# Output projections of two attention loops in three passes of high and low parts, next to the value projection

## The reference, cut to what matters

```python
x = x + tanh(g_xattn[0]) * L0_xattn(layernorm(x), ctx)      # q from x, k and v from ctx; W_proj, b_proj
x = x + tanh(g_ffn[0])   * L0_ffn(layernorm(x))             # top-1 of 8 experts, capacity, gelu
x = x + tanh(g_xattn[1]) * L1_xattn(layernorm(x), ctx, ctx) # wq, wk, wv, wo
x = x + tanh(g_ffn[1])   * L1_ffn(layernorm(x))             # top-2 of 4 experts
```

## Time and profile before

| | us |
|---|---|
| median of 3 runs | 2356.29 (2355.44 to 2358.41) |
| profiled execution | 2359.46 |
| its span | 2357.7 |
| PE busy | 2199.6 (93%) |
| DVE busy | 1744.6 (74%) |
| POOL busy | 1228.8 (52%) |
| ACT busy | 1193.6 (51%) |

### The profile page before, as it was taken

One profiled execution on the slowest core, in us unless ns is written; L12 is line 12 of the kernel. 1 busy time (PEld: TensorE's weight loads), 2 busy tenths in 40 slices (PEclk: granted clock), 3 DMA queues, 4 the chain that ended last, 5 costly groups with the idle time before them and its releaser, 6 DMA issues.

```text
span 2357.7 us, 55177 instructions
## 1 busy us (share of the span) xinstructions
PE 2199.6 (93%) x18512; PEld 1816.8 (77%) x18512; DVE 1744.6 (74%) x4727; ACT 1193.6 (51%) x2389; POOL 1228.8 (52%) x2200
## 2 busy tenths in 40 slices
PE   4999999999599999999969999999789999999997
PEld 3887787787488888888858888888667777777775
DVE  2788888888456666575558877878668888888885
ACT  2655555555333332333336666666556656666663
POOL 2666776776300000000056666666258888888886
PEclk9999999999799999999979999999989999999998
DMA  8112122112212222221122222222200000000000
GB/s 265 44 60 64 57 62 64 57 62 89 110 36 92 87 80 92 74 91 38 45 70 68 69 72 71 67 67 91 93 12 28 28 28 27 27 28 31 27 23 17
DMA packets 125388, 148.06 MB, mean 63 GB/s; under 512 B 13834, under 2 KB 117522, under 8 KB 122772
## 3 DMA queue, kind: packets, MB, share of 16 engines
q1 hardware_dynamic: 119060, 128.84, 17.0%
q0 software_dynamic: 6144, 16.79, 2.2%
HBM read 86.86 MB, written 58.72 MB: 62 GB/s over the span
## 4 chain that ended last, share of the span: by engine, by line
PE 73%; DVE 9%; POOL 8%; issue 4%; ACT 2%; SPq 2%; DMA 1%; POOLq 0%; ACTq 0%; DVEq 0%
PE ps L1095 11%; PE ps L974 10%; PE ps L1109 8%; PE ps L959 5%; PE ps L1039 5%; PE ps L913 4%; PE ps L1111 4%; PE ps L1058 4%; PE ps L1177 4%; DVE u2g L1481 3%; PE ps L1006 3%; PE ps L930 2%; PE ps L1132 2%; PE ps L907 2%; DVE h_st L1450 2%
## 5 line engine op out<-in xcount | busy, mean ns | idle before, releaser
L1229 DVE TENSOR_REDUCE nmax<-ps 128x16 f32<-128x2048 f32 x128 | 293.3, 2291 | 62.0 <-PE ps L930 61.9
L826 ACT ACTIVATE hid<-ps,b_in 128x512 f32<-128x512 f32 x192 | 132.5, 690 | 361.6 <-PE ps L1095 338.7
L592 POOL COPY slot_in<-slot_all 128x1 int32 (+1 forms) x64 | 11.4, 178 | 567.6 <-DMA eo_d<-eo 567.6
L784 ACT ACTIVATE prob_t<-ps 128x2048 f32<-128x2048 f32 x128 | 240.5, 1879 | 76.9 <-PE ps L913 76.9
L1109 PE MATMUL ps<-w_hl,hid_hi 128*128 128x512 f32 x768 | 269.5, 396 | 0.0
L1095 PE MATMUL ps<-xgt_hi,w_hl 128*128 128x512 f32 x768 | 243.8, 394 | 1.5 <-DVE xgt_lo L1382 1.5
L1177 PE MATMUL ps<-w2f,a_t 128*128 128x256 f32 x1024 | 244.2, 382 | 0.0
L1177 PEld LDWEIGHTS ps<-w2f,a_t 128*128 128x128 f32 x1024 | 196.3, 192 | 27.7
L1111 PE MATMUL ps<-w_hl,hid_lo 128*128 128x256 f32 x768 | 212.9, 277 | 0.0
L863 ACT ACTIVATE z<-ps,h_rs 128x256 f32<-128x256 f32 x256 | 123.7, 563 | 165.4 <-POOL h_rs L696 165.4
L566 POOL TENSOR_TENSOR km_r<-qk,cst 128x512 fp32r<-128x512 f32 x128 | 133.4, 1042 | 130.1 <-ACT qk L774 130.0
(11 more groups left out here) (196 smaller groups left out, 6038.5 us busy)
## 6 DMA issues: line engine op xcount, KB each, us to landing
c_t<-in_ctx_in_dram SPq DMA_DIRECT2D x128, 128.0 KB, 2.1
x_d<-x SPq DMA_DIRECT2D x128, 128.0 KB, 2.1
w_raw<-in_w_dram SPq DMA_DIRECT2D x16, 1024.0 KB, 7.9
slots_d<-zeros SPq DMA_DIRECT2D x12, 1024.0 KB, 9.3
xg<-slots_d SPq DMA_DIRECT2D x24, 512.0 KB, 4.7
eo_d<-eo SPq DMA_DIRECT2D x24, 512.0 KB, 3.2
x_in<-in_x_dram SPq DMA_DIRECT2D x64, 128.0 KB, 2.1
x_in<-x_d SPq DMA_DIRECT2D x64, 128.0 KB, 2.3
```

The costliest lines, as they stand in the source:

```text
L784: nc.scalar.activation(prob_t[:].rearrange("p a k -> p (a k)"), scores.rearrange("p a k -> p (a k)"), ACT.Exp, scale=SOFT).then_inc(y["exp ...
L826: nc.scalar.activation(hid[:, fc % 2, :], ps[:, 4 + fc % 2, 0:G], ACT.Gelu, bias=b1_in[:, e.parity, fc:fc + 1]).then_inc(z["hid_done"].sem, 1)
L1229: nc.vector.tensor_reduce(nmax[:, b.parity, :, 0:4], scores.rearrange("p a (r k) -> p a r k", k=P), AX_X, ALU.max, negate=True).then_inc(y ...
```

## The change

The output projection takes high and low parts in float32r, in three passes, as the value projection does. In both loops:

- ACT makes `o_hi` behind `o_t`, from the same PSUM bank; POOL makes `o_lo = o_t - o_hi` behind the bias (loop 0) or the gather (loop 1), ahead of `km_r`. PE waits for `o_lo` in place of `o_t`.
- PE's output projection stands behind the turning of `xh`, directly ahead of the value projection, and has six matmuls.
- POOL's `c_lo` moves from ahead of `km_r` and `qm` to behind them, ahead of the scatter.
- `w_v` and `w_p` share one buffer, `w_vp`. The output weights are loaded in SP's step -1, once `wv_lo` is made; ACT scales them and makes `wp_hi` at the end of its step 1, DVE makes `wp_lo` at the end of its step 2. PE waits for three weights ahead of the loop, and for `wp_lo` ahead of its first output projection.
- `xh`, `x_t` and `o_n` have one buffer each in place of two, and wait for the batch before in place of the one before that.

```diff
@@ SP
-                for dst, src in ((w_q, wq), (w_k, wk), (w_v, wv), (w_p, wp)):
+                for dst, src in ((w_q, wq), (w_k, wk), (w_vp, wv)):
...
+                    if s.known and s.off == -1:
+                        sp.wait_ge(s_wv[n], 2)
+                        sp.dma_start(w_vp[:], wp[n]).then_inc(s_w[n], 16)
@@ POOL
-                    b = s - 1
-                    if b.within(B):
-                        pool.wait_ge(y["c_hi_done"].of(b), y["c_hi_done"].at(b))
+                    b = s - 4
+                    if b.within(B):
+                        pool.wait_ge(y["o_t_done"].of(b), y["o_t_done"].at(b))
                         if (b - 2).begun:
-                            pool.wait_ge(y["v_done"].of(b - 2), y["v_done"].at(b - 2))
-                        nc.gpsimd.tensor_tensor(c_lo[:, b.parity], c_t[:, b.off % 4], c_hi[:, b.parity], ALU.subtract)\
-                            .then_inc(y["c_lo_done"].sem, 1)
+                            pool.wait_ge(y["pr_done"].of(b - 2), y["pr_done"].at(b - 2))
+                        nc.gpsimd.tensor_tensor(o_lo[:, b.parity], o_t[:, b.parity], o_hi[:, b.parity], ALU.subtract)\
+                            .then_inc(y["o_lo_done"].sem, 1)
                     b = s
...
                         masked(qm[:, b.parity], qk[:, b.off % 4, 0:2, :]).then_inc(y["qm_done"].sem, 1)
+                    b = s - 1
+                    if b.within(B):
+                        pool.wait_ge(y["c_hi_done"].of(b), y["c_hi_done"].at(b))
...
+                        nc.gpsimd.tensor_tensor(c_lo[:, b.parity], c_t[:, b.off % 4], c_hi[:, b.parity], ALU.subtract)\
+                            .then_inc(y["c_lo_done"].sem, 1)
@@ ACT
-                act.wait_ge(s_w[n], 64)
-                nc.scalar.activation(w_p[:], w_p[:], ACT.Copy, scale=g_t[:, n:n + 1]).then_inc(s_wp[n], 1)
-                nc.scalar.activation(wv_hi[:], w_v[:], ACT.Copy).then_inc(s_wv[n], 1)
+                act.wait_ge(s_w[n], 48)
+                nc.scalar.activation(wv_hi[:], w_vp[:], ACT.Copy).then_inc(s_wv[n], 1)
...
                         nc.scalar.activation(o_t[:, b.parity].rearrange("p a k -> p (a k)"), b4[:, 0:D], ACT.Copy).then_inc(y["o_t_done"].sem, 1)
+                        nc.scalar.activation(o_hi[:, b.parity].rearrange("p a k -> p (a k)"), b4[:, 0:D], ACT.Copy).then_inc(y["o_t_done"].sem, 1)
...
+                    if s.known and s.off == 1:
+                        act.wait_ge(s_w[n], 64)
+                        nc.scalar.activation(w_vp[:], w_vp[:], ACT.Copy, scale=g_t[:, n:n + 1]).then_inc(s_wp[n], 1)
+                        act.wait_ge(s_wp[n], 1)
+                        nc.scalar.activation(wp_hi[:], w_vp[:], ACT.Copy).then_inc(s_wp[n], 1)
@@ PE
-                    b = s - 4
-                    if b.within(B):
-                        pe.wait_ge(y["o_t_done"].of(b), y["o_t_done"].at(b))
...
-                            mm = pe.matmul(b6[:, 0:D], o_t[:, b.parity, c, :], w_p[:, c, :], start=(c == 0), stop=(c == C - 1))
-                        mm.then_inc(y["pr_done"].sem, 1)
                     b = s + 1
...
                         mm.then_inc(y["x_turned"].sem, 1)
+                    b = s - 4
+                    if b.within(B):
+                        pe.wait_ge(y["o_lo_done"].of(b), y["o_lo_done"].at(b))
...
+                        if b.known and b.off == 0:
+                            pe.wait_ge(s_wp[n], 3)
+                        for c in range(C):
+                            for ot, w in ((o_hi, wp_hi), (o_hi, wp_lo), (o_lo, wp_hi)):
+                                mm = pe.matmul(b6[:, 0:D], ot[:, b.parity, c, :], w[:, c, :],
+                                               start=(c == 0 and ot is o_hi and w is wp_hi), stop=(c == C - 1 and ot is o_lo))
+                        mm.then_inc(y["pr_done"].sem, 1)
@@ DVE
+                    if s.known and s.off == 2:
+                        dve.wait_ge(s_wp[n], 2)
+                        nc.vector.tensor_tensor(wp_lo[:], w_vp[:], wp_hi[:], ALU.subtract).then_inc(s_wp[n], 1)
```

More of the change, by code:

```diff
@@ L216, in flamingo_gated @@
         w_k = sb("w_k", [P, C, D])
-        w_v = sb("w_v", [P, C, D])
+        w_vp = sb("w_vp", [P, C, D])
         wv_hi = sb("wv_hi", [P, C, D], F32R)
         wv_lo = sb("wv_lo", [P, C, D], F32R)
-        w_p = sb("w_p", [P, C, D])
+        wp_hi = sb("wp_hi", [P, C, D], F32R)
+        wp_lo = sb("wp_lo", [P, C, D], F32R)
         bp_g = sb("bp_g", [P, D])
@@ L241, in flamingo_gated @@
         rs1 = psb("rs1", [P, 2])
-        xh = psb("xh", [P, 2, D])
-        x_t = psb("x_t", [P, 2, C, P])
+        xh = psb("xh", [P, D])
+        x_t = psb("x_t", [P, C, P])
         x2_t = psb("x2_t", [P, C, P])
@@ L251, in flamingo_gated @@
         rden = psb("rden", [P, H])
-        o_n = psb("o_n", [P, 2, H, DH])
+        o_n = psb("o_n", [P, H, DH])
         o_t = psb("o_t", [P, 2, C, P])
+        o_hi = psb("o_hi", [P, 2, C, P], F32R)
+        o_lo = psb("o_lo", [P, 2, C, P], F32R)
         x1 = psb("x1", [P, 4, D])
@@ L738, in step @@
                         act.wait_ge(y["x_turned"].of(b), y["x_turned"].at(b))
-                        if (b - 2).begun:
-                            act.wait_ge(y["qk_done"].of(b - 2), y["qk_done"].at(b - 2))
-                        nc.scalar.activation(x_t[:, b.parity].rearrange("p a k -> p (a k)"), b7[:, P:P + D], ACT.Copy)\
+                        if (b - 1).begun:
+                            act.wait_ge(y["qk_done"].of(b - 1), y["qk_done"].at(b - 1))
+                        nc.scalar.activation(x_t[:].rearrange("p a k -> p (a k)"), b7[:, P:P + D], ACT.Copy)\
                             .then_inc(y["x_t_done"].sem, 1)
@@ L897, in _ @@
                 y = sy[n]
-                pe.wait_ge(s_w[n], 64)
-                pe.wait_ge(s_wp[n], 1)
+                pe.wait_ge(s_w[n], 48)
                 pe.wait_ge(s_wv[n], 2)
@@ L943, in step @@
                             mm = pe.transpose(b4[:, c * P:(c + 1) * P],
-                                              o_n[:, b.parity].rearrange("p h d -> p (h d)")[:, c * P:(c + 1) * P], ident)
+                                              o_n[:].rearrange("p h d -> p (h d)")[:, c * P:(c + 1) * P], ident)
                         mm.then_inc(y["o2_done"].sem, 1)
@@ L984, in step @@
                             pe.wait_ge(y["qk_out"].of(b - 1), y["qk_out"].at(b - 1))
-                        projections(w_q, 0, x_t[:, b.parity])
+                        projections(w_q, 0, x_t)
                         pe.wait_ge(y["c_came"].of(b), y["c_came"].at(b))
@@ L1032, in step @@
                             mm.then_inc(y["lg_done"].sem, 1)
-                    b = s - 4
-                    if b.within(B):
-                        pe.wait_ge(y["o_t_done"].of(b), y["o_t_done"].at(b))
-                        if not (b + 1).within(B):
-                            pe.wait_ge(y["x1_done"].of(b - 1), y["x1_done"].at(b - 1))
-                        for c in range(C):
-                            mm = pe.matmul(b6[:, 0:D], o_t[:, b.parity, c, :], w_p[:, c, :], start=(c == 0), stop=(c == C - 1))
-                        mm.then_inc(y["pr_done"].sem, 1)
                     b = s + 1
@@ L1046, in step @@
                         for c in range(C):
-                            mm = pe.transpose(b7[:, (1 + c) * P:(2 + c) * P], xh[:, b.parity, c * P:(c + 1) * P], ident)
+                            mm = pe.transpose(b7[:, (1 + c) * P:(2 + c) * P], xh[:, c * P:(c + 1) * P], ident)
                         mm.then_inc(y["x_turned"].sem, 1)
+                    b = s - 4
+                    if b.within(B):
+                        pe.wait_ge(y["o_lo_done"].of(b), y["o_lo_done"].at(b))
+                        if not (b + 1).within(B):
+                            pe.wait_ge(y["x1_done"].of(b - 1), y["x1_done"].at(b - 1))
+                        if b.known and b.off == 0:
[5 more added lines that the diff above has]
+                        mm.then_inc(y["pr_done"].sem, 1)
                     b = s - 2
@@ L1220, in _ @@
                 dve.wait_ge(s_wv[n], 1)
-                nc.vector.tensor_tensor(wv_lo[:], w_v[:], wv_hi[:], ALU.subtract).then_inc(s_wv[n], 1)
+                nc.vector.tensor_tensor(wv_lo[:], w_vp[:], wv_hi[:], ALU.subtract).then_inc(s_wv[n], 1)
                 def step(s):
@@ L1233, in step @@
                         dve.wait_ge(y["n1_rstd"].of(b), y["n1_rstd"].at(b))
-                        if (b - 2).begun:
-                            dve.wait_ge(y["x_turned"].of(b - 2), y["x_turned"].at(b - 2))
+                        if (b - 1).begun:
+                            dve.wait_ge(y["x_turned"].of(b - 1), y["x_turned"].at(b - 1))
                         src = x_in if n == 0 else x2
-                        nc.vector.tensor_scalar(xh[:, b.parity, :], src[:, b.off % 8, :], mv1[:, 0:1], rs1[:, 1:2], ALU.subtract, ALU.mult)\
```

(8 more changed lines are left out.)

6 lines of the change are left out of this document (5 added, 1 removed).

## The result

The changed kernel takes 2377.22 us (median of 4 runs, 2376.68 to 2384.37), the kernel before 2357.35 beside it: a ratio of 1.0091, 95% interval 1.0069 to 1.0112. It is slower, by 20 us, where 2349.5 was forecast, between 2341 and 2360. The profiled execution took 2384.37 us, a span of 2382.6.

The account below looks back on a forecast made before the run. PE was taken to bound the kernel (73% of the chain, loop 1 without a gap). Terms -9.7 + 1.6 - 1.0 + 2.0 + 0.3 = -6.8 us took the profiled 2359.46 to 2352.7, median 2349.5; range 2341 to 2360.

Parts of the forecast that it names:

- the term 59 x 0.165: Loop 1: the shorter projection saves PE 0.165 us in each of 59 steps, -9.7 us.
- 7.42 forecast: Loop 1: PE's step was to take 7.42 us, from 7.587 before.
- 0.7 forecast: Loop 1: POOL was to keep 0.7 us of slack before `km_r`, with `o_lo` ahead of it.
- The DVE prices: Loop 0: DVE waits out the moved `c_lo`, +0.19 us in the `onehot` step and +0.43 in the `slot_s` step.
- +0.125: Loop 0: change of a four-step pattern in us, -3 x 0.165 + 0.19 + 0.43; 13 patterns give +1.6.
- +1.07 for 1.1: Ends of both loops: `o_hi` and `o_lo` delay the last projection by 1.1 us, less 0.1 for its shortening; +2.0 in all.
- The rival of the half-clock stretches: Loop 0: longer PE stalls bring up to nine more stretches at clock 0.50, 13 to 15 us: 2362 to 2365; chance 0.14.
- the first rival: Loop 0: DVE's small operations slip in ahead of `c_lo`, blocking costs nothing, 8 us more saved: 2341.5; chance 0.13.
- 2352.7 forecast: Whole kernel: time forecast for the profiled execution, from 2359.46 before.
- the sum: Whole kernel: all terms of both loops, their starts and ends together, -6.8 us.

Follow-up runs that it names:

- e8_old_place: e4_span4 with PE's six projection matmuls put back at their old place ahead of the turning of `xh`; 2361.58 us.
- e1_unrolled: The changed kernel with PE's steps of loop 1 written out, without a loop instruction; 2354.67 us.
- e2_shift128: The changed kernel with 128 more instructions, long-satisfied waits, at PE's very start; 2356.84 us.
- e4_span4: The changed kernel with PE's loop in loop 1 turning every four steps instead of eight; 2355.70 us.
- e6_c_lo_second: The changed kernel with PE's loop of four steps and POOL's `c_lo` moved between `o_lo` and `km_r`; 2338.26 us.
- e3_before_shift84: The kernel before the change with 84 more instructions, long-satisfied waits, at PE's start; 2388.14 us.

## Why the prediction was wrong

**The step that failed** is the one that opens it: that in loop 1 "each microsecond that PE's instructions lose is a microsecond of the result, until another engine ends later", and with it the term 59 x 0.165. It priced PE's work and every engine's waits, and nothing for the bringing of PE's instructions. The change adds 16 matmuls and 16 weight loads to a body of eight steps. That body has 8 x 95 = 760 matmuls before (5512 in 58 steps) and 8 x 97 = 776 after (583 in the six steps above), with as many weight loads and some 76 other instructions: 1596 and 1628, or 6.2 and 6.4 packets. The steps written out ahead of it grow by four instructions a batch, 64 x 4 = 256 in loop 0, which is a whole packet and moves nothing, and some 50 in loop 1. The body's end so moves some 83 instructions on, its start some 50, and with that, over a boundary: a body of either length touches seven packets or eight, by its place. That seven stay and eight do not is inferred, since no view shows where the boundaries lie. But it gives every shift its result (84, 128, 256 and the change itself) if the body of before starts between some 115 and 170 instructions behind a boundary. No rival held this. That the kernel before fell on the right side was luck, and 84 idle instructions take it over (2388 us).

The trace of before had the sign, q8 silent from turn to turn; it says that the body just has to fit, and I did not ask by how much it does. The Trainium skill ("Runtime: NRT & Kernel Launch", Instruction fetch mechanics) says that a taken branch breaks the sequential prefetch and stalls when its target is not among the resident pages, and it gives PE room for 2048 instructions in blocks of 256. The runs agree with the mechanism. They add that a body of 1628, under that room, misses or not by where it lies (2377.22 us as it was, 2356.84 with 128 instructions ahead of it); the same section's window of two pages is not what is seen, since 1596 instructions jumped back without a fetch.

**What was right.** Six matmuls take 0.80 us with the first longer distance, and the step is 7.43 us for 7.42 forecast; PE is not idle before L949, and POOL keeps 0.83 us before `km_r` (0.7 forecast). The DVE prices hold to a hundredth. The `onehot` step, of the earlier trace rows, after:

```profile
364.20 1.04 POOL L572 TENSOR_TENSOR qm<-qk,cst 128x512 f32<-128x512 f32 x1
364.32 0.96 DVE L1308 SCALAR_TENSOR_TENSOR firsts<-diff,cst 128x32 f32<-128x32 f32 x1
365.19 0.72 POOL L634 TENSOR_TENSOR c_lo<-c_t,c_hi 128x256 fp32r<-128x256 f32 x1
365.54 0.43 DVE L1316 TENSOR_TENSOR onehot<-firsts,first 128x32 bf16<-128x32 f32 x1
366.02 0.19 PE L1038 MATMUL ps<-onehot,tri 128*128 128x40 bf16 x1 [1.61 <-DVE onehot L1316]
```

`onehot` is 0.43 for 0.24 and PE's stall 1.61 for 1.42, as forecast. The `slot_s` step, of the earlier trace rows:

```profile
382.31 0.90 DVE L1287 TENSOR_SCALAR far<-kept 128x4 f32<-128x4 f32 x1
383.13 0.74 POOL L634 TENSOR_TENSOR c_lo<-c_t,c_hi 128x256 fp32r<-128x256 f32 x1
383.82 0.15 DVE L1293 CAST slot_all<-slot_f 128x4 f32 x1
```

`slot_all` starts 0.61 us behind the end of `far`, 0.19 before: 0.42 later, 0.43 forecast. An undisturbed pattern went from 34.83 to 34.76, where +0.125 was said, because ordinary steps of loop 0 lost 0.23 us (8.22 to 7.99), not 0.165: 0.16 by the passes and 0.07 by the place, as e8_old_place shows (8.06). The last projection, of the earlier trace rows, in the chain of waits:

```profile
1722.53 0.38 ACT o_t L762
1722.91 0.28 ACT o_hi L763
1723.19 0.07 issue
1723.26 0.73 POOL o_lo L618
1724.00 0.04 issue
1724.04 1.39 PE ps L1069 x6
```

From `o_t` to the projection 1.51 us, 0.44 before: +1.07 for 1.1.

**What was mis-sized.** The rival of the half-clock stretches was the right mechanism for loop 0 and came in at two stretches more, not five: 3 us. Its worth is seen from the other side. With `c_lo` ahead of the masked keys the kernel takes 2338.3, less than the 2341.5 that the first rival gave to a `c_lo` that holds up nothing: the stretches of before go too, 4 x 1.5 us, which I had not counted. And a wait of 1.7 us stands once in loop 1 (below).

Without the stalls the profiled executions take 2353.46 (e1_unrolled), 2353.37 (e2_shift128) and 2353.96 (e4_span4), for 2352.7 forecast. The medians are 2354.7 to 2356.8, not 2349.5: I had taken 3.2 us off for the profiled run of before lying that far above its median, and that distance does not carry over to another kernel. So the agreement with 2352.7 is in part luck: one execution of before that was long is set beside executions that were short for theirs. Median against median, the three save 0.3 to 2.5 us where the sum said 6.8. By medians alone, then, the change with its body well placed is no faster than what can be told apart; its gain in loop 1 (60 steps, 9.2 us) is eaten in loop 0 by a moved instruction of another engine.

**The best version** is e6_c_lo_second: three passes beside the value projection, `c_lo` ahead of the masked keys, PE's loop of four steps. 2338.26 us, 0.79% under before (0.9921, 0.9908 to 0.9935), and 39 us under the change as made: 21 from the turns, 17 from `c_lo`.

## What to carry to other kernels

A loop on an engine whose body fills several instruction packets can turn for nothing or for 7 us, and an edit that adds instructions anywhere ahead of it decides which: look for instruction packets between the first turn and the last, and keep the body well under what stays resident (half the steps cost nothing here). When an operation of POOL is moved, read which DVE operations on SBUF will stand behind it, and what PE's stall then does to its clock. And price a change against profiles of the same execution; do not move a profile's distance from its median over to the next kernel.

## What the runs showed of the hardware

A turn that misses costs PE twice: it was idle for 4.5 us in the first one and then ran at 1.2 GHz for 6.8 us. 9 packets came for a body of 6.4.

DVE can wait out not one POOL instruction but a chain of them. In e1_unrolled, once in loop 1:

```profile
1545.53 0.74 POOL L618 TENSOR_TENSOR o_lo<-o_t,o_hi 128x256 fp32r<-128x256 f32 x1
1545.68 3.55 DVE L1337 SCALAR_TENSOR_TENSOR rows<-y_in,wgt_all,x_in 128x256 f32<-128x256 f32 x1
1546.21 1.04 POOL L572 TENSOR_TENSOR km_r<-qk,cst 128x512 fp32r<-128x512 f32 x1
1547.21 1.04 POOL L572 TENSOR_TENSOR qm<-qk,cst 128x512 f32<-128x512 f32 x1
1548.21 0.72 POOL L634 TENSOR_TENSOR c_lo<-c_t,c_hi 128x256 fp32r<-128x256 f32 x1
```

The DVE operation starts while `o_lo` runs and ends at 1549.23, 0.3 us behind `c_lo`: four instructions back to back. One step earlier it starts with `km_r`, takes 1.34 us and ends 0.3 us behind `km_r` alone. `o_n` is late by it and PE stands 1.57 us. The same wait is in every version of the change at that step. What makes POOL late there stands in the kernel before too, where it cost nothing: its gather comes behind 2.0 us of idle time instead of 0.55.

```profile
1547.69 1.12 POOL L596 DMA_INDIRECT y_in<-eo_d,slot_in  x1 [1.99 <-issue]
```

Why that one gather is late is not shown. The Trainium skill ("SBUF — State Buffer", Who interferes with whom) speaks of a lock held for one instruction; here, as the times read, it passed from one POOL instruction to the next with DVE waiting. In e6_c_lo_second `c_lo` stands ahead of `km_r`, and DVE starts under it:

```profile
1529.65 0.73 POOL L625 TENSOR_TENSOR c_lo<-c_t,c_hi 128x256 fp32r<-128x256 f32 x1
1529.81 2.85 DVE L1337 SCALAR_TENSOR_TENSOR rows<-y_in,wgt_all,x_in 128x256 f32<-128x256 f32 x1
```

It ends 0.3 us behind `qm`, the last of a chain of three (`c_lo`, `km_r`, `qm`), and the step loses 1.0 us instead of 1.7.

What stays open: why, at the alignment of the changed kernel, a turn misses in some executions and not in others (two to four of four in the profiled ones), while e3_before_shift84 missed all four in its profiled execution and its four times lie within 2 us of each other; and where the boundaries of the packets lie.
